# Graph attention with one set of scores: scores computed once and exponentials turned on TensorE

## What is computed

```python
def layer0(x, adj, ...):                       # x (16, 512, 256), adj (16, 512, 512)
    q, k, v = proj(Wq, bq), proj(Wk, bk), proj(Wv, bv)          # 8 heads of 32
    scores = einsum('bhqd,bhkd->bhqk', q, k) / sqrt(32)
    scores = where(adj + eye > 0, scores, -inf)
    attn = softmax(scores, axis=-1)
    out = einsum('bhqk,bhkd->bhqd', attn, v) @ Wo.T + bo
    h = x + out
    return layernorm(h) * gamma + beta

def layer1(feats, adj, ...):
    f = feats @ fc_w.T + fc_b
    logits = (f @ q_w.T + q_b) + (f @ k_w.T + k_b).T
    masked = logits + (1 - adj) * -1e9
    masked = where(masked >= 0, masked, 0.01 * masked)
    return softmax(masked) @ f + feats
```

## Time and profile before

| | |
|---|---|
| median of 3 runs | 1097.93 us (1094.98 to 1108.29) |
| the profiled execution | 1106.9 us, span of its instructions 1104.8 us |
| mean granted TensorE clock | 0.971 of full speed |
| share of the span busy: TensorE, VectorE, GpSimd, ScalarE | 92%, 71%, 65%, 56% |

### The profile page before, as it was taken

One profiled execution on the slowest core, in us unless ns is written; L12 is line 12 of the kernel. 1 busy time (PEld: TensorE's weight loads), 2 busy tenths in 40 slices (PEclk: granted clock), 3 DMA queues, 4 the chain that ended last, 5 costly groups with the idle time before them and its releaser, 6 DMA issues. The chain is left out here.

```text
span 1104.8 us, 16668 instructions
## 1 busy us (share of the span) xinstructions
PE 1021.8 (92%) x5720; PEld 649.2 (59%) x5720; DVE 782.6 (71%) x1945; ACT 622.8 (56%) x1180; POOL 722.8 (65%) x415
## 2 busy tenths in 40 slices
PE   5789899999999999999999998999999999999866
PEld 4445565656656565665666564666656566665454
DVE  4667777877767787777778777777767767775432
ACT  2145466565646557575655657564555746566633
POOL 3056787675667667666777766576766657778740
PEclk9899999999999999999999999999989999999978
DMA  5677827576564667667374767646366663745010
GB/s 133 106 123 145 133 73 143 102 144 96 113 116 89 135 113 144 96 121 127 102 134 83 153 115 137 103 103 119 79 141 105 136 108 99 135 76 90 29 48 28
DMA packets 81571, 120.89 MB, mean 109 GB/s; under 512 B 9296, under 2 KB 36432, under 8 KB 81488
## 3 DMA queue, kind: packets, MB, share of 16 engines
q1 hardware_dynamic: 81488, 119.84, 56.8%
HBM read 52.44 MB, written 8.39 MB: 55 GB/s over the span
## 5 line engine op out<-in xcount | busy, mean ns | idle before, releaser
L708 ACT ACTIVATE e<-st_bank 128x512 f32<-128x512 f32 x512 | 307.4, 602 | 404.1 <-PE st_bank L526 223.5
L928 DVE CUSTOM_DVE_ANT_0 sm_bank<-sm_bank,masks 128x512 f32<-128x512 f32 x512 | 354.1, 693 | 155.3 <-PE sm_bank L534 152.2
L1009 POOL TENSOR_TENSOR e_sum<-e_sum,e 128x1024 f32<-128x1024 f32 x128 | 303.7, 2385 | 49.8 <-ACT e L708 49.8
L534 PE MATMUL sm_bank<-kt_hi,q_pad 128*128 128x512 f32 x512 | 281.9, 552 | 32.9 <-issue 28.0
L524 PE MATMUL st_bank<-q_stack,k_stack 97*128 97x512 f32 x432 | 197.7, 458 | 3.8 <-ACT e L708 3.0
L1009 POOL TENSOR_TENSOR e_sum<-e 128x1024 f32<-128x1024 f32 x64 | 152.2, 2378 | 67.9 <-ACT e L708 61.1
L526 PE MATMUL st_bank<-mask_t,ident_b 128*128 128x512 bf16 x432 | 169.2, 392 | 0.0
L524 PEld LDWEIGHTS st_bank<-q_stack,k_stack 97*128 97x128 f32 x432 | 81.5, 189 | 111.5 <-ACT e L708 103.3
L462 PE MATMUL o_bank<-e,v 128*32 128x512 f32 x1024 | 136.4, 605 | 0.7 <-ACT e L708 0.7
L505 PE MATMUL shared<-feat,z 128*128 128x256 f32 x512 | 134.5, 412 | 1.4 <-ACT z L651 1.4
L534 PEld LDWEIGHTS sm_bank<-kt_hi,q_pad 128*128 128x128 f32 x512 | 103.2, 202 | 44.5 <-issue 31.8
(11 more groups left out here) (131 smaller groups left out, 1836.7 us busy)
## 6 DMA issues: line engine op xcount, KB each, us to landing
adj_in<-in_adj SPq DMA_DIRECT2D x32, 1024.0 KB, 7.8
q_stack<-qt_hi SPq DMA_DIRECT2D x64, 256.0 KB, 9.7
k_stack<-kt_hi SPq DMA_DIRECT2D x64, 256.0 KB, 8.8
x_in<-in_x SPq DMA_DIRECT2D x16, 512.0 KB, 10.4
q_pad<-qt_hi SPq DMA_DIRECT2D x128, 64.0 KB, 7.7
q_stack<-qt_lo SPq DMA_DIRECT2D x32, 256.0 KB, 8.6
k_stack<-kt_lo SPq DMA_DIRECT2D x32, 256.0 KB, 11.9
h<-in_x SPq DMA_DIRECT2D x16, 512.0 KB, 3.8
```

Source lines behind the costliest of these rows:

```text
L534: nc.tensor.matmul(sm_bank[s % 2][:, :], q_pad[j // GH][:, j % GH, qt * P:(qt + 1) * P], kt_hi[j // GH][:, :], start=True, stop=True).then ...
L708: nc.scalar.activation(e[:, kt, i, :], st_bank[s % 2][:, :], ACT.Exp, scale=SCALE)\
L928: nc.vector.tensor_tensor_reduce(sm_bank[s % 2][:, :], sm_bank[s % 2][:, :], mask[nxt if off else par][:, qt * N:(qt + 1) * N], 1.0, LOWES ...
L1009: nc.gpsimd.tensor_tensor(e_sum[:, pair, :], a, b, ALU.add).then_inc(pool_done.sem, 1)
```

## The change

The stacks have 96 rows and hold -q times the scale, so the scores come out negated. Each tile (head, query block) is computed once, into one of three `sm_bank` (`SCORED`). VectorE adds the mask (now +2^100 where there is no edge) and takes the row *minimum* in the same instruction, and writes the masked tile back to PSUM. ScalarE takes exp(minimum - tile) from there with the row sum as a second output. VectorE takes the reciprocal of 128 sums one position later (`RECIP`), and GpSimd multiplies the 128x512 tile by it, in place. TensorE transposes the scaled tile in four pieces of 128x128 into one of two `et_bank`, three positions later (`TURN`), and ScalarE, or VectorE in the eight tiles of `DVE_COPIED`, copies it into `e_t`. `times_v` takes half of a group's queries at a time: four blocks of 16 matmuls of 256 columns in place of eight blocks of four of 512. `e` is a ring of four tiles (`ROOM`). Padding, the transposed mask, transposed maxima, the sums by ones, the wide reciprocals and the multiplication of the output are gone; the low part of the output is made by VectorE from `o_bank`. Two banks are left for all fills, in turn. The gamma, beta, bias and layer 1 mask passes of GpSimd are cut into one instruction for each of four row blocks. All positions stand in new tables (`PE_AT`, `ACT_AT`, `DVE_AT`, `POOL_AT`, `SP_AT`), where a value of 32 k + s means position s, k iterations after that of the batch's scores.

```diff
-DVE_MASKED = (12, 14, 15, 26, 29)
-LEAD = 21
+TURN = 3
+ROOM = 4
+RECIP = 1
+SCORED = 3
+TURNED = 2
+SHARED = 2
+DVE_COPIED = (7, 8, 17, 18, 19, 21, 26, 28)
...
+PE_AT = {
+    "q1": 2, "et2": 67, "pv3": 36, "at2": 69, "at3": 70, "op1": 39, "op0": 40, "v0": 8, "v1": 10, "xt0": -21, "xt1": -20,
...
-        shared = [pb(f"shared{i}") for i in range(3)]
-        bank_of = {name: shared[n % 3] for n, name in enumerate(FILLS)}
+        shared = [pb(f"shared{i}") for i in range(SHARED)]
+        bank_of = {name: shared[n] for name, n in BANK.items()}
...
+            def times_v(k, b):
...
+                for kt in range(NT):
                     for i in range(GH):
                         o = g * P + i * DH
...
+                        last = nc.tensor.matmul(o_bank[i * DH:(i + 1) * DH, 2 * half * P:2 * (half + 1) * P], v[:, kt, o:o + DH],
+                                                e_t[:, k % 2, kt, i, :], start=(kt == 0), stop=(kt == NT - 1))
...
+            def scores(s, b):
+                g, i, qt = tile(s)
+                if s % (TILES // NG) == 0:
+                    pe.wait_ge(stacked[g].sem, stacked[g].of(f"stack{g}", b))
+                u, earlier = ago(s, SCORED)
+                pe.wait_ge(exp_done.sem, exp_done.of(u, b + earlier))
+                nc.tensor.matmul(sm_bank[(TILES * b + s) % SCORED][:, :], q_stack[g][:, i, qt * P:(qt + 1) * P], k_stack[g][:, i, :],
+                                 start=True, stop=True).then_inc(sm_done.sem, 1)
+
+            def turn(u, b):
+                pe.wait_ge(scaled.sem, scaled.of(u, b))
+                w, earlier = ago(u, TURNED)
+                copied = dve_copied if w in DVE_COPIED else act_copied
+                pe.wait_ge(copied.sem, copied.of(w, b + earlier))
+                n = TILES * b + u
+                for c in range(NT):
+                    last = nc.tensor.transpose(et_bank[n % TURNED][:, c * P:(c + 1) * P], e[:, n % ROOM, c * P:(c + 1) * P], ident[:, :])
+                last.then_inc(turned.sem, 1)
...
+            def exponential(s, b):
+                u, earlier = ago(s, ROOM)
+                act.wait_ge(min_done.sem, min_done.of(s, b))
+                act.wait_ge(turned.sem, turned.of(u, b + earlier))
...
+                nc.scalar.activation(e[:, k, :], sm_bank[n % SCORED][:, :], ACT.Exp, scale=-1.0, bias=row_min[:, k:k + 1],
+                                     accum_out=row_sum[:, k:k + 1]).then_inc(exp_done.sem, 1)
...
+            def normalise(s, b):
+                pool.wait_ge(recip_done.sem, recip_done.of(s, b))
+                k = (TILES * b + s) % ROOM
+                nc.gpsimd.tensor_scalar(e[:, k, :], e[:, k, :], row_recip[:, k:k + 1], None, ALU.mult).then_inc(scaled.sem, 1)
```

More of the change, by code:

```diff
@@ L36 @@
 DT = D // P
-POS = NG * NT * GH
+TILES = NH * NT
+PAIRS = 4
 SCALE = float(DH) ** -0.5
@@ new lines, in build @@
+        recip_done = Signal(sem("recip_done"), [ago(s, RECIP) for s in range(TILES)])
+        scaled = Signal(sem("scaled"), tiles)
+        turned_tiles = [ago(s, TURN) for s in range(TILES)]
+        turned = Signal(sem("turned"), turned_tiles)
+        act_copied = Signal(sem("act_copied"), [u for u in turned_tiles if u[0] not in DVE_COPIED])
+        dve_copied = Signal(sem("dve_copied"), [u for u in turned_tiles if u[0] in DVE_COPIED])
+        pe_done = Signal(sem("pe_done"), steps(PE_AT))
@@ L225, in build @@
+        stacked = [Signal(sem(f"stacked{g}"), [step for step in loads if step[0] == f"stack{g}"], 16 * 6) for g in range(NG)]
+        stored = [Signal(sem(f"stored{i}"), [step for step in loads if step[0] == f"store{i}"], 16) for i in range(2)]
         weights_loaded, cols_loaded, const_loaded = sem("weights_loaded"), sem("cols_loaded"), sem("const_loaded")
@@ new lines, in attend @@
+            def attend(c, b):
+                k = c % 2
+                pe.wait_ge(act_done.sem, max(act_done.of(f"et{c}", b), act_done.all("feat", b)))
+                if k == 0:
+                    pe.wait_ge(*bank_read(f"at{c}", b))
+                bank = bank_of[f"at{c}"]
+                for kt in range(NT):
+                    last = nc.tensor.matmul(bank[:, k * D:(k + 1) * D], z[:, c, kt * P:(kt + 1) * P], feat[:, kt, :],
+                                            start=(kt == 0), stop=(kt == NT - 1))
+                last.then_inc(pe_done.sem, 1)
@@ new lines, in o_high, with normal_rows @@
+            def o_high(g, b):
+                act.wait_ge(pe_done.sem, max(pe_done.of("kb", b - 1), pe_done.all("fc", b - 1)))
+                copy(o_hi[:, g, :], f"pv{2 * g + 1}", o_bank[:, :], b)
+            def normal_rows(half, b):
+                act.wait_ge(pool_done.sem, pool_done.of("shift", b))
+                for c in range(2 * half, 2 * half + 2):
+                    last = nc.scalar.activation(h[b % 2][:, c, :], h[b % 2][:, c, :], ACT.Identity, bias=shift[:, c:c + 1],
+                                                scale=rstd[:, c:c + 1])
+                last.then_inc(act_done.sem, 1)
@@ new lines, in statistics, with combine @@
+            def statistics(half, b):
+                dve.wait_ge(dve_done.sem, dve_done.of(f"h_add{half}", b))
+                for c in range(2 * half, 2 * half + 2):
+                    last = nc.vector.bn_stats(stats[:, c, :], h[b % 2][:, c, :])
+                last.then_inc(done, 1)
+            def combine(b):
+                dve.wait_ge(dve_done.sem, dve_done.all("stats", b))
+                for c in range(NT):
+                    last = nc.vector.bn_aggr(moments[:, c, :], stats[:, c, :])
+                last.then_inc(done, 1)
@@ new lines, in query_logits @@
+            def query_logits(half, b):
+                dve.wait_ge(act_done.sem, act_done.of(f"feat{half}", b))
+                dve.wait_ge(pe_done.sem, pe_done.all("at", b - 1))
+                for k in range(2):
+                    c = 2 * half + k
+                    last = nc.vector.tensor_tensor_reduce(z[:, c, 0:D], bank_of[f"fc{half}"][:, k * D:(k + 1) * D], qw_row[:, :],
+                                                          1.0, logit_bias[:, 3:4], ALU.mult, ALU.add, q_dot[:, c:c + 1])
+                last.then_inc(done, 1)
@@ new lines, in layer1_maxima @@
+            def layer1_maxima(half, b):
+                dve.wait_ge(dve_done.sem, dve_done.all("q_dot", b))
+                dve.wait_ge(pe_done.sem, pe_done.of("kb", b))
+                dve.wait_ge(pool_done.sem, max(pool_done.of(f"l_mask{2 * half + k}", b) for k in range(2)))
+                for k in range(2):
+                    c = 2 * half + k
+                    last = nc.vector.tensor_tensor_reduce(z[:, c, 0:N], bank_of["kb"][:, :], adj_in[:, c, :], 1.0, LOWEST,
+                                                          ALU.add, ALU.max, z[:, c, N:N + 1])
+                last.then_inc(done, 1)
```

1172 lines of the change are left out of this document (527 added, 645 removed), and 31 rows, old and new, of tables (ACT_AT, ACT_STEPS, DVE_AT, DVE_STEPS).

## The result

The changed kernel takes **1176.56 us** (median of 4 runs, 1175.0 to 1177.4) against 1097.62 us before in the same comparison: a ratio of 1.068, 95% interval 1.0625 to 1.0735. The forecast was 1013 us with a range to 1105. The time went the other way and left the range.

The account below looks back on a forecast made before the run. TensorE, 97% busy in the middle, bounds at 64.0 us a batch; 4.1 less gives 59.9. Over 16 batches -66 us, start -15, end -5: span 1019, execution 1021, at 0.992 a median of 1013 us, range 985 to 1105.

Parts of the forecast that it names:

- the price of GpSimd's product: GpSimd's 128x512 product by a column: 0.65 us each, 20.8 for 32, putting GpSimd at 34 us a batch.
- with 1.29 it is 55, still under TensorE: GpSimd's batch total if each product took 1.29 us: 55 us, still less than TensorE's.
- TensorE's sum: TensorE per batch: 18.1 us removed, 14.0 added for turned tiles, net 4.1 less; 64.0 becomes 59.9, other losses kept.
- ScalarE 52 and VectorE 49 us: Busy time a batch after the change: ScalarE from 38.4 to 52 us, VectorE from 48.3 to 49.
- The chain: Exponential, reciprocal, product, turn, copy, next exponential: 3.1 us for three positions lasting 5.6, so 2 us of fills fit.
- Start and end: First exponential's scores at 38 us instead of 53.5, -15 us; last scores to first output projection shorter, -5 us.
- In series: Rival: fills add to the chain once three positions of slack are used up; 70 us a batch, 1173 us; chance 0.13.
- Queues eat half: Rival: queues at two shared banks and ScalarE's heap cost 3 us a batch; 63 a batch, 1061 us; chance 0.25.
- no net gain: Rival: dear `times_v` weights (3.2) and part of the turns' 5.2 take back the 4.1; about 1093 us; chance 0.13.
- The heap of positions 19 to 24: ScalarE's work there, in the queues rival: 11.7 us, while TensorE has 9.8.
- The clock: Rival: turns at 1.2 GHz would take 14.0 us more a batch, 1237 us; chance 0.04.
- What would show it: Signs: right, groups 60 us apart and TensorE 95% busy; wrong, TensorE idle before scores or turns, product over 1.3 us.

Follow-up runs that it names:

- tile of ones: Changed kernel with GpSimd's product replaced by a two-input multiplication by a full tile of ones, weights left unnormalised: 1076.82 us, ratio 0.9787.
- two-operation kernel: Changed kernel with a second operation, times 1.0, filled in on GpSimd's product by the column, result whole: 982.8 us, ratio 0.8932.
- side loads: Two-operation kernel plus a GpSimd instruction behind each product, on tiles nobody waits for: two operations on 512 columns 1061.6 us; one on 256 columns 1136.22 us.
- the one with 1.053: Changed kernel with GpSimd's product made a two-input operation, the column of reciprocals read with a step of zero, result whole: 1014.33 us, ratio 0.9192.

## Why the prediction was wrong, step by step

- **The step that failed** is the price of GpSimd's product: 0.65, because "one input is what it is", between 0.48 and 1.29. It is 1.575, outside both ends. The pass of L1047, from which the lower end came, has two operations; the trace before has no row of a one-operation pass over a wide tile. The counter-sign was in the kernel text, not in the profile: `None` for the second operation. I took the two-input row as an upper bound because two inputs should cost more than one; the runs show the reverse, 1.502 against 1.295.
- **The second step that failed** stood beside it: "with 1.29 it is 55, still under TensorE", so no cost. At 1.295 (tile of ones) the batch is 62.2 us and not 56.25: 6 us, though GpSimd's sum is 55.3 us. I compared sums of a whole batch. TensorE's work is 2.25 us a position in positions 4 to 10 and 1.6 in the others, and GpSimd can't make up for the 8.2 us in which it idles while TensorE is the slower one.
- **TensorE's sum** held, and was too cautious. The net 4.1 us less came out as 62.2 - 56.1 = 6.1 of busy time in the two-operation kernel, and its waits of 1.8 us a batch went as well, which the forecast kept: 7.75 us in all. Of the 2.0 us beyond the forecast some 1.2 are the clock, by an estimate: the middle before ran at a granted 0.98 and this one at 1.00, and 62.2 x 0.98 is 61.0. Another 0.8 are the turns, at 0.41 us and not 0.44.
- **ScalarE 52 and VectorE 49 us** held: 52 and 48. The exponential's step was taken as 0.68; in ScalarE's timeline it is 0.68 (608.08 to 608.76, exponential to copy), though the group has 0.695 and another 0.207 for reading the sum.
- **The chain** (3.1 us for three positions, with 2 us of cover) cost nothing with the product at 0.7 us: TensorE is then busy for 99.7% of the middle.
- **Start and end:** -15 was -9.7 and -5 was -2.5 in the changed kernel, -9 and -6.3 in the two-operation one. The stack landed some 6 us later than assumed: the first scores waited for the low part of k until 43.8, a little past my bound of 43. The 12 us that the forecast took for the end are more than its own terms, 6.5 + 2 x 1.72 = 9.9.
- **The rivals.** "In series" gave 1173 us, nearly the time that came, by a mechanism that isn't the main one: it put the waits into positions 7 to 12, but there TensorE is busy throughout (only position 11 waits, 0.9 us), and with the same chain and a cheap product nothing waits. A fifth of the loss is, by the side loads, the length of a tile's way. "Queues eat half" and "no net gain" didn't come: TensorE waits for the copies of turned tiles for 0.3 us in all, and not at all before scores. The heap of positions 19 to 24 was also summed too high: its terms give 11.4 us, not 11.7.
- **The clock.** "TensorE: Matmul & The Clock Gate" of the Trainium skill, Part 4, says that PE-mode transposes don't count as activity for the gate in the same way. The fall that the forecast feared from it didn't come: with 160 transposes a batch the middle is granted 1.00 in the two-operation kernel and 0.99 in the changed one. Whether transposes count as matmuls do, these rows can't tell, since matmuls stand beside them everywhere. Where the clock fell at position 2, TensorE had been busy for 1.8 of 3.5 us, and the two turns among that work are transposes; the two-operation kernel has the same turns without the waits, and no fall there.
- **What would show it** named "a product over 1.3 us", and that was the first line to read. The kernel that comes nearest to the forecast's own price, 0.707 for 0.65, took 983 us, 3% under the 1013. That the one with 1.053 took 1014, the forecast's number, is chance: its price is dearer and TensorE's saving larger than forecast.

## What to carry to other kernels

Take a price from a row whose instruction has the same form, down to the number of operations and inputs, and look into the kernel text for that. Where there is no such row, the price is open, and a row of another form is no bound for it: here the two-input row was taken for one, and the one-input instruction was dearer. When work moves to an engine, compare it with the bounding engine stretch by stretch, not by sums of a batch: what it idles in one stretch it may not make up in the next. And where TensorE waits often, its clock can fall behind the waits and add to them.

## What the runs showed of the hardware

- GpSimd's pass over 128x512 of f32 in SBUF, in place: one operation 1.502 us whether it multiplies or adds a constant, 1.575 with a column; two operations 0.618 to 0.622 with constants and 0.707 with a column and a constant. A second operation that does nothing makes the product by a column 2.2 times faster. One operation on 256 columns takes 0.857.
- GpSimd's two-input product of 128x512 takes 1.295 us with a full tile, 1.053 with one column read for all 512.
- VectorE's one-operation product of that size takes 0.695 us on average, from 0.485 to 0.951.
- TensorE's clock fell behind 3.5 us in which it was busy for 1.8, in one batch of three or in most of them: the next 3.3 to 3.65 us have a granted 0.53 to 0.59 in the windows shown. A fall cost 1.2 to 1.6 us. The same 3.5 us stood ahead of batches without a fall.
